# Attention sums copied from PSUM in two instructions, and closed one unit later

## The reference, cut to what matters

```
feat = (h @ W).reshape(N, H, D)                    # H = 4 heads, D = 64
el, er = sum(feat * al, -1), sum(feat * ar, -1)
e = leaky_relu(el[src] + er[dst], 0.2)
ex = exp(e - segment_max(e, dst)[dst])
den = segment_sum(ex, dst)
out = segment_sum((ex / den[dst])[:, :, None] * feat[src], dst)
```

## Time and profile before

| | us |
|---|---|
| median of three runs | 4582.62 (4581.59 to 4592.7) |
| profiled execution, its time | 4589.54 |
| profiled execution, its span | 4587.8 |
| TensorE matmuls busy, share of the span | 2683.6 (58%) |
| VectorE busy | 3300.8 (72%) |
| ScalarE busy | 2458.8 (54%) |
| first to last PSUM copy, stage 0, 1, 2, 3 | 453.6, 485.1, 479.7, 455.2 |
| mean granted TensorE clock | 0.78 of full speed |

### The profile page before, as it was taken

How to read it: one execution, slowest core, us unless ns; L and a number is a source line. 1 busy time by engine, 2 the same in 40 slices (tenths; PEclk the granted TensorE clock), 3 DMA queues, 4 the chain that set the end, 5 groups by cost and what they waited for, 6 DMA issues and landing times. The chain is left out here.

```text
span 4587.8 us, 75546 instructions
## 1 busy us (share of the span) xinstructions
PE 2683.6 (58%) x26874; PEld 2338.9 (51%) x26874; DVE 3300.8 (72%) x5736; ACT 2458.8 (54%) x4684; POOL 1498.3 (33%) x1226
## 2 busy tenths in 40 slices
PE   2223222058600566564399974889847888639997
PEld 2112111034400334333399874878837888538887
DVE  4999666043300677776799987889977889779997
ACT  3223222000200544442699975878948889669997
POOL 0777788866667777770000000000000000100000
PEclk8555555579855666666799997999978999879999
DMA  6223232266100222220121211121102121012111
GB/s 265 33 33 49 33 33 9 0 159 163 45 17 18 51 50 50 49 46 5 39 71 43 57 33 37 44 71 36 55 5 75 42 64 56 10 39 66 47 56 58
DMA packets 330204, 242.67 MB, mean 53 GB/s; under 512 B 86728, under 2 KB 318410, under 8 KB 328906
## 3 DMA queue, kind: packets, MB, share of 16 engines
q1 hardware_dynamic: 246474, 188.80, 14.0%
q0 software_dynamic: 82304, 29.95, 6.8%
q10 hardware_dynamic: 1152, 20.58, 1.1%
HBM read 211.56 MB, written 27.68 MB: 52 GB/s over the span
## 5 line engine op out<-in xcount | busy, mean ns | idle before, releaser
L484 POOL DMA_INDIRECT table<-adj_value,adj_cell x392 | 620.8, 1584 | 198.7 <-issue 190.0
L1462 PE MATMUL g1a_ps<-g_parts,g1a_pos 128*128 128x195 bf16 x2500 | 440.0, 251 | 123.5 <-DVE g1a_side L1574 115.7
L1462 PE MATMUL g2a_ps<-g_parts,g2a_pos 128*128 128x195 bf16 x2500 | 436.8, 250 | 120.9 <-DVE g2a_side L1574 99.8
L985 POOL DMA_INDIRECT l_row<-node_rows,l_rec x416 | 460.4, 1107 | 132.8 <-issue 126.1
L1462 PE MATMUL g3a_ps<-g_parts,g3a_pos 128*128 128x195 bf16 x2500 | 431.4, 248 | 107.5 <-DVE g3a_side L1574 106.5
L1462 PE MATMUL g0a_ps<-g_parts,g0a_pos 128*128 128x195 bf16 x2500 | 430.4, 248 | 105.8 <-DVE g0a_side L1574 104.9
L704 DVE TENSOR_SCALAR_CACHE_REDUCE adj_same<-adj_rows,adj_key 128x1792 bf16<-128x1792 f32 (+1 forms) x392 | 448.7, 1209 | 30.3 <-issue 13.7
L999 PE MATMUL l_ps<-l_value,l_hot 128*128 128x260 f32 x832 | 345.4, 577 | 181.8 <-issue 92.9
L1489 ACT ACTIVATE g1a_side<-g1a_er,g_elb 128x512 f16<-128x512 f32 (+1 forms) x700 | 407.8, 663 | 76.0 <-PE g1a_ps L1464 71.8
L539 PE MATMUL adj_ps<-adj_pair,adj_same 128*128 128x2 bf16 x2940 | 133.7, 165 | 532.8 <-DVE adj_same L704 530.1
L1489 ACT ACTIVATE g2a_side<-g2a_er,g_elb 128x512 f16<-128x512 f32 (+1 forms) x700 | 407.8, 664 | 69.9 <-PE g2a_ps L1464 65.7
(11 more groups left out here) (380 smaller groups left out, 6413.4 us busy)
## 6 DMA issues: line engine op xcount, KB each, us to landing
gcn_cols<-table SPq DMA_DIRECT2D x24, 1600.0 KB, 8.2
adj_rows<-key_rows SPq DMA_DIRECT2D x28, 896.0 KB, 4.4
table<-zeros ACTq DMA_DIRECT2D x8, 2512.5 KB, 27.3
g0a_cols<-table SPq DMA_DIRECT2D x8, 1024.0 KB, 5.5
g1a_cols<-table SPq DMA_DIRECT2D x8, 1024.0 KB, 5.4
g2a_cols<-table SPq DMA_DIRECT2D x8, 1024.0 KB, 6.1
g3a_cols<-table SPq DMA_DIRECT2D x8, 1024.0 KB, 5.4
l_row<-node_rows,l_rec POOLq DMA_INDIRECT x416, 2.6
```

The costliest lines, as they stand in the source:

```text
L484: pool.indirect_dma_start(out=table.rearrange("(w o) -> w o", o=1), out_offset=bass.IndirectOffsetOnAxis(cell[:, u, k:k + 1], 0), in_=valu ...
L985: pool.indirect_dma_start(out=row[:, u, k, :], out_offset=None, in_=node_rows, in_offset=bass.IndirectOffsetOnAxis(rec[:, j, 0:1].bitcast( ...
L1462: pe.matmul(bank[:, 0:HW], pos[:, slot, b - b0, j * P:(j + 1) * P], parts[:, b, 0, k, :], start=(b == 0), stop=False, skip_group_check=True)
```

## The change

- `evacuate` takes a half: half 0 copies banks 0 and 1, half 1 the rest (two banks in a wide item, one in a narrow one). Half 0 is issued after the signs of unit 2 of the next item, half 1 after those of unit 4. Before, one copy stood after unit 3.
- `evacuated` counts two per item, so its waits and its start value are doubled.
- VectorE's closing steps move back by one slot: `add_middle` behind unit 5, `add_low` behind unit 6, then `scale`, `both`, `invert`, `divide` and `add` behind units 0 to 4 of the item after. The steps that follow the last unit of a stage grow by one `scale`.

```diff
@@ TensorE, item()
-                pe.wait_ge(evacuated, n + 1)
+                pe.wait_ge(evacuated, n * 2 + 2)
@@ ScalarE
-            def evacuate(n):
+            def evacuate(n, half):
                 act.wait_ge(masks_free, MASKS + (n + 1) * NU)
                 act.wait_ge(taken_free, n + 1)
-                nblk = WIDTHS[n // H]
-                act.copy(taken[:, n % 2, 0:nblk, :], ps[:, GB * (n % 2):GB * (n % 2) + nblk, 0:2 * HW]).then_inc(evacuated, 1)
-            act.sem_inc(evacuated, 2)
+                lo, hi = (0, 2) if half == 0 else (2, WIDTHS[n // H])
+                act.copy(taken[:, n % 2, lo:hi, :], ps[:, GB * (n % 2) + lo:GB * (n % 2) + hi, 0:2 * HW]).then_inc(evacuated, 1)
+            act.sem_inc(evacuated, 4)
...
-                    if q == 3 and n >= 1:
-                        evacuate(n - 1)
-            evacuate(ITEMS - 1)
+                    if q in (2, 4) and n >= 1:
+                        evacuate(n - 1, q // 2 - 1)
+            evacuate(ITEMS - 1, 0)
+            evacuate(ITEMS - 1, 1)
@@ VectorE
-                dve.wait_ge(evacuated, 2 + n + 1)
+                dve.wait_ge(evacuated, 4 + 2 * (n + 1))
...
                     if n >= 1:
-                        {4: add_middle, 5: add_low, 6: scale}.get(q, lambda n: None)(n - 1)
+                        {5: add_middle, 6: add_low}.get(q, lambda n: None)(n - 1)
                     if n >= 2:
-                        {0: both, 1: invert, 2: divide, 3: add}.get(q, lambda n: None)(n - 2)
-            for part in (both, invert, divide, add):
+                        {0: scale, 1: both, 2: invert, 3: divide, 4: add}.get(q, lambda n: None)(n - 2)
+            for part in (scale, both, invert, divide, add):
                 part(ITEMS - 2)
```

## The result

The changed kernel takes 4611.49 us (median of 6 runs, 4606.85 to 4617.3), the kernel before 4580.81 in the same comparison (6 runs, 4567.96 to 4592.7): ratio 1.0072 [1.0056, 1.0088], slower by 30.7 us. The forecast had 4640 with both of its costs; what came is its rival B, the ring alone, worked out as 4611. The measured time lies in the stated range of 4600 to 4654 only because that range was drawn to take B in; A's own range, 4628 to 4654, misses it. Half of the forecast sum didn't come, so the range held by its width and not by the mechanism that was given 0.55. The profiled execution took 4617.3 us.

What follows compares the result with a forecast made beforehand. A dependency loop through four mask slots (ScalarE, VectorE, TensorE) was taken to set the period. 4582.6 us plus 28.8 for delays in that loop plus 28.8 for instruction-fetch stalls in stage 3 gave 4640 us, range 4600 to 4654.

Steps and rivals of the forecast that it cites:

- rival B: Only the delays in the mask-slot loop come, stage 3 stays inside its seven instruction blocks: 4611 us, chance 0.22.
- A: The forecast itself: mask-slot loop delays plus new instruction-fetch stalls in stage 3, 4640 us, chance 0.55.
- The copy's durations: ScalarE's PSUM copies: 0.13 us fixed plus 0.325 per bank, so 0.78 for two banks and 0.46 for one.
- The narrow term: Narrow items: the first half copy delays unit 3's signs, so TensorE starts unit 2 late, +0.37 to 0.39 us an item.
- The wide term by `scale`: Wide items: `scale` replaces `both` before positive mask 1 on VectorE, so TensorE's unit 0 comes 0.18 us later.
- covered by 0.03, so about nothing: Wide items: with the first half copy, negative mask 2 is done at 13.14 us and TensorE needs it at 13.17.
- The ring's sum: Mask-slot loop delays: 2.5 us from wide and 4.7 from narrow items, 7.2 a stage, +28.8 over four stages.
- stage 3 gains the three stalls: +28.8 us: TensorE's wide loop in stage 3 touches an eighth instruction block and refetches at three jumps back, 9.6 us each.
- Stage 3 is 0.7 us from an eighth block: TensorE's stage 3 loop body ends some 16 instructions before the next fetch edge, by fetch spacing in turn 1.
- C: Only the stage 3 fetch stalls come, masks running ahead absorb both mask-slot loop delays: 4611 us, chance 0.08.
- E: Nothing reaches the critical path: 4583 us, chance 0.05.
- D: Narrow loop: the shorter copy before unit 4 saves 0.33 us an item, the earlier half costs nothing: 4577 us, chance 0.07.

Runs made afterwards that it cites:

- e2: Kernel before with only the two half copies, behind units 2 and 4, VectorE closing where it did: 4610.15 us against 4573.58, ratio 1.008.
- e1: Kernel before with only VectorE's closing one unit later, the copy whole behind unit 3: 4589.5 us against 4573.58, ratio 1.0036.
- e4: Kernel before with the whole copy moved one unit earlier, behind unit 2: 4659.38 us against 4573.58, ratio 1.0191.
- h4: Kernel before with 24 idle TensorE instructions ahead of stage 3's loops, behind the increment freeing the mask slots: 4579.69 us against 4574.48, ratio 1.0009.
- h5: Kernel before with 60 idle TensorE instructions ahead of stage 3's loops, behind the increment freeing the mask slots: 4602.12 us against 4572.0, ratio 1.0056.
- h1: Kernel before with 20, 60 and 64 idle TensorE instructions in stages 1, 2 and 3, behind the increment freeing the mask slots: 4535.62 us, ratio 0.9909.
- f2: Kernel before with 20, 60 and 64 idle TensorE instructions in stages 1, 2 and 3, before the increment freeing the mask slots: 4542.65 us, ratio 0.9935.
- e3: Kernel before with the copy in halves behind units 3 and 4, VectorE closing where it did: 4567.83 us against 4573.58, ratio 0.9987.
- f1: Kernel before with eight idle TensorE instructions ahead of stage 3's loops: 4576.76 us against 4574.30, ratio 1.0005.

## Why the forecast came out as it did

**The copy's durations: right.** 0.79 and 0.46 us, from the fixed part and the bank's part.

**The narrow term, +0.37 to 0.39: right, and shown.** The period grew by 0.38; e2 has it alone, e1 hasn't, e4 enlarges it. Its path (signs of unit 3, positive mask 3, negative mask 2, TensorE's unit 2) stands in the rows above. Unit 2 starts at 10.91 us after the item's start; the forecast's 4441.23 - 4430.33 is 10.90.

**The wide term by `scale`, +0.18: right in size, and e1 has it alone (+0.17).** The sentence beside it, that the first half in a wide item is "covered by 0.03, so about nothing", was right only with the late close in place. Alone it costs as much (e2). The sum didn't suffer, since the two overlap.

**The ring's sum, +28.8: right within 4 us.** Stages 0 and 3 show 7.1 and 7.7 for the 7.2, and with all fetch stalls removed the difference is 25.1 us by medians and 27.8 by the profiles' stages.

**The failed step: "n * 2 + 2 needs a product of its own, at least one register instruction a turn", and from it "stage 3 gains the three stalls: +28.8 us".** The runs show none: the traces of before and after hold equally many TensorE instructions, 26874 matmuls and 30186 others, and 1666 of them from one jump back to the next in either. At the wait, one register instruction gave way to another kind (84 of them in each trace), and none was added. So neither the start nor the length of a loop moved. The number of TensorE instructions was taken from how long the source line is, and a price of 28.8 us hung on it. In its place nothing came: no q8 fetch in turns 2 to 4 of stage 3, and +7.7 us there, which is the ring.

**A second step was off too: "Stage 3 is 0.7 us from an eighth block: [...] some 16 instructions".** With 24 instructions in front the stage doesn't refetch, with 60 it does (h4, h5). The edge had been worked out from the spacing of the fetches in turn 1, and that was too coarse for it. The reading under it was wrong too. The forecast took 7 fetches in turn 1 for a body that touches one block too many, and 6 for one that fits, and said that stage 2 behaves as stage 1. But stage 2 of the kernel before has 6 and refetches, and stage 2 of h1 has 7 and doesn't. What decides is the place, as f2, h1 and h5 show; where exactly the edges lie no run shows. Stage 3 refetches when it stands 60 instructions later, but not at 24 or at 144.

**Rivals.** B is what happened. A falls with the absent q8 in stage 3. C and E fall with the periods, both of which grew by the forecast terms. D needed VectorE to reach mask 3 later than its signs; in after it stands waiting for them, 0.61 us. Its other half is real, though: a shorter stretch in front of unit 4 does pay once nothing in front of unit 3 gets longer (e3, -0.27 a narrow item, where D had 0.33).

**What stays open.** The medians differ by 30.7 us, the profiles' four stages by 21.5, and the medians without fetch stalls by 25.1. Part of what lies between has nothing to do with the change: the two profiled spans differ by 27.7 us, and 3.3 of that lie ahead of stage 0. The rest is put down to stages 1 and 2, whose stalls vary: profiles of stage 2 had three, two or one of them (f1 and h5 two, h4 one). The kernel before scatters over 18 to 25 us from run to run, the versions without fetch stalls over 4 to 14. Taking all the stalls away gave 36 us by medians and 31.8 + 25.7 = 57.5 by the profiles' copies, so unprofiled executions of the kernel before seem to have fewer of them than profiled ones.

The same would account for an excess in all of e1 to e4. By what stages 0 and 3 changed, taken four times, they should be at +9, +26, -15 and +80 us; by medians they are at +16, +37, -6 and +86, 6 to 11 us above each. The traces add a hint. In the profiles of e1 to e4 and of the change, stage 2 fetches seven times in its first turn and has all three stalls. In those of the kernel before, f1, h4 and h5 it fetches six times, and three, two, one and two stalls came. So the change, which alters no place in TensorE's stream, may still make the stalls of stage 2 more regular by its timing. That is argued, not shown: what lets a stall fail to appear in one execution wasn't found.

## What to carry to other kernels

Before an instruction is moved forward in a ring of engines, follow the one that is queued behind it, to the unit which the next engine needs first. Here cutting the copy paid only where its first part stood no earlier than the whole one had, and two delays in one loop were not added where they struck different units. A loop in registers has a place as well as a length: look for refetches at its jumps back, and shift it by a few dozen idle instructions, beside other work, where they show. For any edit of such a program, count the instructions in the compiled stream and don't guess them from the source.

## What the runs showed of the hardware

- A TensorE loop of 1666 instructions ran its later turns without a fetch or with 9 a turn, and experiments that changed only its place turned the one into the other: 455.2 to 475.2 us in stage 3 (h5), and 485.1 to 453.3 in stage 1 (h1). The Trainium skill, "Runtime: NRT & Kernel Launch", section Instruction fetch mechanics, says that a jump to a block no longer held forces a fetch. That agrees with the 27 q8 fetches of h5. Its window of two blocks doesn't agree with the absent q8 in stages 0 and 3.
- A stall at a jump back isn't one price: the item that spans the jump was longer by 10.1 to 10.8 us in stage 1, 8.0 to 9.2 in stage 2 and 6.7 in h5's stage 3. It comes and goes between executions in stage 2.
- Instructions on TensorE that only count up a semaphore followed one another at 0.15 us: 60 of them took 9.0 us in h5, and held the next stage by 7 us in f2.
- The expression n * 2 + 2 in a wait took no more TensorE instructions than n + 1.
